# Gate and up projections of two batches in one product, attention of the last batch moved ahead, activation tables loaded at other places

## The chip, the cores and the metric

The kernel runs on one core of a Trainium2 chip. The metric is the device time of one execution in microseconds, the median of several runs. The core has a matrix engine (TensorE, "PE" in the profile, with its weight loads shown as "PEld"), a vector engine (VectorE, "DVE"), an activation engine (ScalarE, "ACT"), a general engine (GpSimd, "POOL") and a queue that issues DMAs (SyncE, "SP"). TensorE writes to eight accumulation banks (PSUM) of 128 x 512 float32; the other data is in SBUF. The engines each run their own instruction list in order and meet through semaphores.

## The reference

One decoder layer on x of 4 batches x 256 tokens x 256 channels, float32, in three parts, each behind a layer norm and added to the residual:

```
h = layernorm(x)                                  # norm 1
q, k = elu(h Wq + bq) + 1, elu(h Wk + bk) + 1     # 16 heads of 16
v = h Wv + bv
x = x + ((q (k^T v)) / (q sum(k) + eps)) Wo + bo  # linear attention, no mask
s = (ctx Wxq + bxq) (ctx Wxk + bxk)^T / 8         # 256 x 256 per batch, from the context alone
x = x + softmax(where(mask, -inf, s * layernorm(x)))          # norm 2
h = hadamard(layernorm(x) * SU_ug) / 64           # norm 3
u, g = h Wup^T * (scale * 64), h Wgate^T * (scale * 64)       # 1024 wide
x = x + (hadamard(silu(g) * u * SU_dp) / 64) Wdown^T * (scale * 64)
```

## The kernel before

Tokens are held as 8 tiles of 128 (`xs`), two per batch. Every product in float32 is made of rounded halves: an operand is split into a rounded part (`_hi`, a ScalarE copy) and what is left (`_lo`, a subtraction on VectorE or GpSimd), and three of the four combinations are added in a bank. A product with a 256-long contraction so takes 2 x 3 = 6 matmuls (`PASSES`).

TensorE's order is written out by hand. `HEAD` (line 55) lists the steps of the attention of batches 0 to 2 and what starts batch 3. Then a loop over the four batches runs eight steps `gate_up(b, j)` (GU, line 1113), each 128 of the 1024 inner columns: 6 matmuls for the gate, 6 for the up part, with a 128 x 128 weight block held in the array and the 256 tokens of one batch moving through it. The two halves fill one bank. Between these steps stand the steps that `SIDE` (line 61) names for (b, j): `ST` and `NUM` (state and numerator of the attention), `AT` (transposes), `OUT` (output projection), `T3` (transposes of the third norm), `XH` (Hadamard of the input), `WD` (Hadamard of the down weights, four matmuls of 512 columns per `pre` part, line 1095). For j = 8 and 9 they stand inside `down(b)` (line 1127), which contracts the eight inner blocks in 48 matmuls into two banks `Y`. For the last batch `down` takes its blocks in an order of its own, so that it need not wait for the last of them.

Seven banks are used in rotation in the order that `schedule()` (line 78) gives: the n-th group of results takes bank n mod 7, and TensorE waits in `take` until the group seven places before it has been read. The eighth bank holds the scores and the softmax (`probs`).

Each gate and up step is followed by a chain: ScalarE's `silu(n)` (line 511, reads the gate half into one of four buffers `sg`), VectorE's `hidden(n)` (line 820, multiplies by the up half and releases the bank), ScalarE's `h_hi(n)` (line 521), GpSimd's `h_lo(n)` (line 312), and TensorE's `down`. `silu(n)` waits for `h_lo(n-4)`, since there are four buffers.

The attention of a batch goes on with VectorE's `attend` (line 726, division), TensorE's `AT`, `at_hi` on ScalarE (line 458), `at_lo` on VectorE (line 674), `OUT`, `add_attn` (line 742), the statistics `ln_stats(2, b)` (line 637), GpSimd's `rstd_of(2, b)` (line 258), `times_score` (line 750), `logits` (line 763), ScalarE's `prob` (line 478), VectorE's `softmax` (line 774) and `ln_stats(3, b)`. Then GpSimd's `rstd_of(3, b)` and `shift_of(3, b)`, ScalarE's `normalise(3, b)` (line 421), `T3`, `x3_hi` and `x3_lo` (lines 486, 783), `XH`, `xh_hi` and `xh_lo`, and the batch is ready for its gate and up steps. `add_y(b)` (line 828) adds the down result to the residual, and SP stores it.

Where these stand among the `hidden`, `silu` and `h_lo` of the loop is written out in each engine's list. Before: `NUM(3)`, `AT(3)` and `OUT(3)` are in batch 1's steps, `XH(2)` too, `T3(3)` and `XH(3)` in batch 2's.

ScalarE holds one set of function tables at a time; exp and silu are in different sets. The loads (`ACT_TABLE_LOAD`) are placed by the compiler in front of the first instruction that needs another set, here the first exp, silu(0), prob(2), silu(8), prob(3) and silu(16).

Of the kernel before, what the change touches and what calls it, by code (L numbers as in the profile page):

```python
# [5 lines left out]
F32 = mybir.dt.float32  # L6
# [7 lines left out]
P = 128  # L14
# [45 lines left out]

SIDE = {(0, 0): (("ST", 3),), (0, 1): (("NUM", 2),), (0, 2): (("T3", 1),), (0, 3): (("WD", 0), ("WD", 1)),
# [12 lines left out]
def banks_of(group, i):  # L74
    return [(group, i, t) for t in range(2)] if group in ("NUM", "Y") else [(group, i, 0)]


def schedule():

    order = [g for name, i in HEAD for g in banks_of(name, i)]  # L80
    for b in range(BATCH):
        for j in range(JB):
            order += [("GU", JB * b + j, 0)]
            order += [g for name, i in SIDE.get((b, j), ()) for g in banks_of(name, i)]
        order += banks_of("Y", b)
        order += [g for j in (JB, JB + 1) for name, i in SIDE.get((b, j), ()) for g in banks_of(name, i)]
    return [g for g in order if g not in (("SC", 0, 0), ("SC", 1, 0))]


def decoder_kernel(nc, x, ctx_t, w_qkv, bias, w_o, w_ug, w_d, vec, row, mask_ss, mask_key, const, out):  # L90
# [8 lines left out]
    with stack:  # L99
        def sb(name, shape, dt=F32):  # L100
            return stack.enter_context(nc.sbuf_tensor(name, shape, dt))
# [9 lines left out]
        wqkv = sb("wqkv", [P, 2, 3, FB, HID], F32R)  # L111
        wo = sb("wo", [P, 2, FB, HID], F32R)
# [20 lines left out]
        exp_first = sb("exp_first", [P, TILES])  # L133
        xn = sb("xn", [P, 2, ST, HID])
# [30 lines left out]
        hs = sb("hs", [P, 2, JB, SEQ], F32R)  # L165

# [12 lines left out]
        junk = back[:, 1, 0:CHUNK // 2].bitcast(BF16)  # L179
        stage = [home[:, i, :].rearrange("p (f c) -> p f c", f=FB) for home in (front, back) for i in range(2)]  # L180
# [23 lines left out]
        def wait_read(eng, name, i, t=0):  # L204
# [12 lines left out]
                 "x3_hi xh_hi sg h_hi h_lo").split()  # L217
# [37 lines left out]
        def _(pool):  # L255
# [60 lines left out]

            g.memset(junk, 0.0).then_inc(s["junk"], 1)
# [32 lines left out]
            for n in range(JB):  # L350
                h_lo(n)
                if n == 1:
                    add_ob(2)
                if n == 4:
                    add_ob(3)
            rstd_of(2, 2)
            rstd_of(3, 2)
            shift_of(3, 2)
            for n in range(JB, 2 * JB):
                h_lo(n)  # L360
                if n == JB + 4:
                    rstd_of(2, 3)
            rstd_of(3, 3)
            shift_of(3, 3)
            for n in range(2 * JB, 4 * JB):
                h_lo(n)
# [4 lines left out]
        def _(act):  # L371
# [4 lines left out]
            a.activation(exp_first[:, :], mhalf[:, :], ACT.Exp)  # L376

# [150 lines left out]

            one_rows()
# [69 lines left out]
            for n in range(JB, 2 * JB):  # L599
                silu(n)  # L600
                if n == JB:
                    normalise(3, 2, xn3)
                else:
                    h_hi(n - 1)
                if n == JB + 2:
                    x3_hi(2)
                if n == JB + 3:
                    at_hi(3)
                if n == JB + 6:
                    xh_hi(2)  # L610
            h_hi(2 * JB - 1)
            prob(3)
            negate_mean(3, 3)
            for n in range(2 * JB, 3 * JB):
                silu(n)
                if n > 2 * JB:
                    h_hi(n - 1)
                if n == 2 * JB + 1:
                    normalise(3, 3, xn3)
                if n == 2 * JB + 3:  # L620
                    x3_hi(3)
                if n == 2 * JB + 5:
                    xh_hi(3)
            h_hi(3 * JB - 1)
            for n in range(3 * JB, 4 * JB):
                silu(n)
                if n > 3 * JB:
                    h_hi(n - 1)
            h_hi(4 * JB - 1)
# [4 lines left out]
        def _(dve):  # L634
# [274 lines left out]
            hidden(7)  # L909
            add_attn(2)  # L910
            ln_stats(2, 2)
            times_score(2)
            logits(2)
            softmax(2)
            ln_stats(3, 2)
            add_y(0)
            for n in range(JB, 2 * JB):
                hidden(n)
                if n == JB + 1:
                    attend(3)  # L920
                if n == JB + 2:
                    x3_lo(2)
                if n == JB + 3:
                    at_lo(3)
                if n == JB + 4:
                    add_attn(3)
                    ln_stats(2, 3)
                    times_score(3)
                if n == JB + 5:
                    logits(3)  # L930
                if n == JB + 6:
                    xh_lo(2)
            softmax(3)
            add_y(1)
            ln_stats(3, 3)
            for n in range(2 * JB, 3 * JB):
                hidden(n)
                if n == 2 * JB + 3:
                    x3_lo(3)
                if n == 2 * JB + 5:  # L940
                    xh_lo(3)
            add_y(2)
            for n in range(3 * JB, 4 * JB):
                hidden(n)
            add_y(3)
# [4 lines left out]
        def _(pe):  # L950
# [7 lines left out]
            def done(ins, name, i, t=0):  # L958
                ins.then_inc(full[bank_of[name, i, t]], 1)
# [166 lines left out]

            def down(b):
# [6 lines left out]
                def block_products(i, j):  # L1134
                    for n, (wa, hb) in enumerate(((1, 0), (0, 0), (0, 1))):
                        ins = mm(dst[i][:, 0:HID], hs[:, hb, j, i * P:(i + 1) * P], wdh[:, wa, j, :],  # L1136
                                 start=(j == 0 and n == 0), stop=(j == JB - 1 and n == 2))
                    return ins

                if b == BATCH - 1:  # L1140

                    for j in range(JB - 1):
                        pe.wait_ge(s["h_lo"], JB * b + j + 1)
                        block_products(0, j)
                    block_products(1, 0)
                    block_products(1, 1)
                    pe.wait_ge(s["h_lo"], JB * b + JB)
                    done(block_products(0, JB - 1), "Y", b, 0)
                    for j in range(2, JB - 1):
                        block_products(1, j)  # L1150
                    done(block_products(1, JB - 1), "Y", b, 1)
                    return
# [17 lines left out]
            for b in range(BATCH):  # L1170
# [4 lines left out]
                down(b)  # L1175

# [42 lines left out]
```

## Time and profile before

| | us |
|---|---|
| device time, median of 3 runs (132.08 to 132.5) | 132.26 |
| span of the profiled execution | 130.6 |
| TensorE busy | 123.9 (95%) |
| VectorE busy | 79.7 (61%) |
| ScalarE busy | 75.4 (58%) |
| GpSimd busy | 68.8 (53%) |

The span runs from the first to the last instruction that the profiler recorded; the device time has the launch and the end around it. Matmuls overlap, so their busy time is no measure of their pace; the pace is the distance from one to the next. "Busy" of an engine is a share of the whole span, and says nothing of a single stretch.

### The profile page before, as it was taken

What the parts mean: (1) busy time and instruction counts of PE and PEld (TensorE: products, weight loads), DVE (VectorE), ACT (ScalarE), POOL (GpSimd) and SP (SyncE); (2) the same over time, 40 slices, a digit from 0 to 9 for tenths busy, and PEclk for the clock granted to TensorE, in tenths of its full rate; (3) what the DMA queues carried; (4) which work ended last, traced back from release to release, by engine and by line L of the source; (5) the groups of instructions that cost most, each with busy time, mean ns of one, the idle gap of its engine ahead of it and who ended that gap; (6) DMA issues with size and microseconds to landing.
All of it is one profiled execution on the core that took longest, in us unless ns stands there. A gap on an engine that the chain in (4) does not pass through costs nothing.

```text
span 130.6 us, 2612 instructions
## 1 busy us (share of the span) xinstructions
PE 123.9 (95%) x974; PEld 116.0 (89%) x974; DVE 79.7 (61%) x202; ACT 75.4 (58%) x162; POOL 68.8 (53%) x89
## 2 busy tenths in 40 slices
PE   6899999996999999999999999999999999999991
PEld 2249799986999999699999999999999999999990
DVE  1279969677997794999786486662535512232211
ACT  1497639984576589668553883556496630345500
POOL 2200999889999998746270344452326350055500
PEclk9999999999999999999999999999999999999999
DMA  4999985000000000000000200000200000200011
GB/s 113 304 346 381 397 241 201 0 0 3 3 5 0 0 0 8 0 0 0 5 0 0 80 0 5 3 0 0 85 0 0 3 0 5 80 0 0 0 39 47
DMA packets 4353, 7.68 MB, mean 59 GB/s; under 512 B 560, under 2 KB 2096, under 8 KB 4212
## 3 DMA queue, kind: packets, MB, share of 16 engines
q1 hardware_dynamic: 4334, 7.50, 17.0%
q8 instruction: 8, 0.13, 0.4%
q14 instruction: 5, 0.04, 0.1%
q10 hardware_dynamic: 6, 0.01, 0.0%
HBM read 6.46 MB, written 1.05 MB: 57 GB/s over the span
## 4 chain that ended last, share of the span: by engine, by line
PE 60%; POOL 13%; DVE 11%; ACT 7%; issue 4%; DMA 3%; POOLq 0%; ACTq 0%
PE bank L1123 31%; PE bank L1136 18%; POOL wd_a L303 4%; POOL wug L309 4%; DMA x_res<-in_x 3%; PE bank L1003 3%; POOL rstd L263 2%; DVE st L644 2%; PE bank L1087 2%; PE bank L1109 2%; PE bank L1025 2%; POOL wd_b L303 2%; PE bank L1069 1%; ACT L518 1%; DVE xT L802 1%
## 5 line engine op out<-in xcount | busy, mean ns | idle before, releaser
L1123 PE MATMUL bank<-xh_home,wug 128*128 128x256 f32 x384 | 49.5, 285 | 0.3 <-DVE at L737 0.3
L1123 PEld LDWEIGHTS bank<-xh_home,wug 128*128 128x128 f32 x384 | 47.1, 191 | 0.9 <-issue 0.7
L314 POOL TENSOR_TENSOR hs<-front,hs 128x256 fp32r<-128x256 f32 x32 | 24.0, 758 | 33.1 <-ACT hs L527 33.1
L518 ACT ACTIVATE front<-bank,vecs 128x256 f32<-128x256 f32 x32 | 15.0, 472 | 20.3 <-PE bank L1123 20.1
L825 DVE SCALAR_TENSOR_TENSOR front<-bank,sc_up,front 128x256 f32<-128x256 f32 x32 | 15.2, 480 | 18.2 <-ACT front L518 18.2
L1136 PE MATMUL bank<-wdh,hs 128*128 128x256 f32 x192 | 23.7, 283 | 0.0
L1136 PEld LDWEIGHTS bank<-wdh,hs 128*128 128x128 f32 x192 | 23.3, 191 | 0.0
L527 ACT CAST hs<-front 128x256 fp32r<-128x256 f32 x32 | 12.8, 400 | 4.0 <-DVE front L825 4.0
L1025 PE MATMUL bank<-wqkv,xT 128*128 128x256 f32 x96 | 14.1, 288 | 0.1
L1025 PEld LDWEIGHTS bank<-wqkv,xT 128*128 128x128 f32 x96 | 12.2, 189 | 1.2 <-ACT xT L436 0.7
L261 POOL TENSOR_SCALAR veps<-mv 128x2 f32<-128x2 f32 x12 | 2.3, 192 | 19.8 <-DVE mv L647 19.1
L644 DVE BATCH_NORM_STATS2 st<-x_res 128x6 f32<-128x256 f32 x24 | 9.0, 416 | 3.3 <-DMA x_res<-in_x 3.1
L303 POOL TENSOR_TENSOR wd_b<-wd_a 128x1024 f32<-128x1024 f32 x4 | 9.5, 2400 | 0.1
L263 POOL TENSOR_TENSOR rstd<-veps,mhalf 128x2 f32<-128x2 f32 x12 | 8.8, 732 | 1.0
L832 DVE TENSOR_TENSOR x_res<-bank,x_res 128x256 f32<-128x256 f32 x8 | 3.1, 419 | 8.8 <-PE bank L1136 8.7
L1049 PE MATMUL bank<-xT,wqkv 128*128 128x256 f32 x48 | 7.0, 285 | 0.0
L483 ACT ACTIVATE bank<-bank,low 128x256 f32<-128x256 f32 x8 | 3.5, 443 | 5.7 <-DVE low L770 5.7
L1087 PE MATMUL bank<-wo,aT 128*128 128x256 f32 x48 | 6.4, 282 | 0.0
L1049 PEld LDWEIGHTS bank<-xT,wqkv 128*128 128x128 f32 x48 | 6.2, 189 | 0.0
L1087 PEld LDWEIGHTS bank<-wo,aT 128*128 128x128 f32 x48 | 5.9, 189 | 0.0
L770 DVE CUSTOM_DVE_ANT_0 bank<-bank,mbias,rstd 128x256 f32<-128x256 f32 x8 | 3.6, 490 | 3.2 <-POOL rstd L263 3.2
L429 ACT ACTIVATE xn<-x_res,nmr,rstd 128x256 f32<-128x256 f32 x6 | 3.3, 594 | 3.6 <-POOL nmr L270 3.6
(105 smaller groups left out, 194.1 us busy)
## 6 DMA issues: line engine op xcount, KB each, us to landing
wd_a<-in_w_d SPq DMA_DIRECT2D x1, 1024.0 KB, 8.6
front<-in_w_ug SPq DMA_DIRECT2D x2, 512.0 KB, 9.7
back<-in_w_ug SPq DMA_DIRECT2D x2, 512.0 KB, 5.0
out<-x_res SPq DMA_DIRECT2D x8, 128.0 KB, 1.9
wd_b<-in_w_qkv SPq DMA_DIRECT2D x3, 256.0 KB, 4.9
x_res<-in_x SPq DMA_DIRECT2D x1, 512.0 KB, 6.6
x_res<-in_x SPq DMA_DIRECT2D x1, 385.0 KB, 3.8
back<-in_ctx_t SPq DMA_DIRECT2D x1, 260.0 KB
```

The source lines that it names most:

```text
L263: g.tensor_tensor(rstd[:, n - 1, two], veps[:, n - 1, two], mhalf[:, 0:2], ALU.pow).then_inc(s[f"rstd{n}"], 1)
L303: g.tensor_tensor(dst[:, :, half, :], src[:, :, 0, :], src[:, :, 1, :], ALU.subtract if half else ALU.add)\
L314: g.tensor_tensor(hs[:, 1, n % JB, :], sg[:, n % RING, :], hs[:, 0, n % JB, :].bitcast(F32), ALU.subtract)\
L518: a.activation(sg[:, n % RING, :], B("GU", n)[:, 0:SEQ], ACT.Silu, scale=vecs[:, V_WSUG + JB + j:V_WSUG + JB + j + 1]).then_inc(s["sg"], 1)
L527: a.copy(hs[:, 0, n % JB, :], sg[:, n % RING, :]).then_inc(s["h_hi"], 1)
L644: v.bn_stats(st[:, n - 1, t, :], xs[:, t, :]).then_inc(s[f"stats{n}"], 1)
L825: v.scalar_tensor_tensor(sg[:, n % RING, :], B("GU", n)[:, SEQ:2 * SEQ], sc_up[:, j:j + 1], sg[:, n % RING, :], ALU.mult, ALU.mult).then_i ...
L1025: ins = mm(into, xT[:, b % 2, xb, k, i * P:(i + 1) * P], wqkv[:, wa, c, k, :], start=(n == 0), stop=(name == "V" and n == len(X_PASSES) - 1))
L1049: mm(into, wqkv[:, wa, 2, k, m * P:(m + 1) * P], xT[:, b % 2, xb, k, :], start=(n == 0), stop=False)
L1087: ins = mm(dst[:, i * HID:(i + 1) * HID], aT[:, ab, k, i * P:(i + 1) * P], wo[:, wa, k, :], start=(n == 0), stop=(n == len(X_PASSES) - 1))
L1123: ins = mm(dst[:, n * SEQ:(n + 1) * SEQ], wug[:, wa, k, at_col + j * P:at_col + (j + 1) * P], xh[b][:, xb, k, :], start=(i == 0), stop=(i ...
L1136: ins = mm(dst[i][:, 0:HID], hs[:, hb, j, i * P:(i + 1) * P], wdh[:, wa, j, :], start=(j == 0 and n == 0), stop=(j == JB - 1 and n == 2))
```

## The change

Batches 0 and 1 (`ALONE = 2`) keep their loop. Batches 2 and 3 (`PAIR`) get eight steps `gate_up_pair(j)`: 12 matmuls each, with the tokens of both batches, 512 columns, moving through one weight block. Gate and up fill a bank each (`GG`). `silu_pair`, `hidden_pair`, `h_hi_pair` and `h_lo_pair` follow; the first two work on 512 columns, the other two on each batch by itself. The two `down` of these batches stand behind all eight steps. Batch 3's inner blocks lie in the memory of the attention weights (`watt`), which are no longer needed, and the four buffers `sg2` in that of the staged gate and up weights. For the pair, batch 2 and 3 must both be through their `XH`: so `NUM(3)` and `OUT(2)` move up into batch 0's steps, `AT(3)` into `down(0)`, `OUT(3)`, `T3(2)`, `XH(2)`, `T3(3)` into batch 1's, `XH(3)` into `down(1)`. The lists of VectorE, ScalarE and GpSimd are put in a matching order: both softmaxes stand in front of the first `hidden` and `silu` of batch 1. `table(...)` is an activation of one column without any other use; it stands before `negate_mean(3, 1)` with silu and behind silu(7) with exp.

```diff
 SIDE = {(0, 0): (("ST", 3),), (0, 1): (("NUM", 2),), (0, 2): (("T3", 1),), (0, 3): (("WD", 0), ("WD", 1)),
-        (0, 4): (("AT", 2), ("WD", 2), ("WD", 3)), (0, 5): (("XH", 1),), (0, 7): (("OUT", 2),),
-        (1, 1): (("NUM", 3),), (1, 2): (("T3", 2),), (1, 3): (("AT", 3),), (1, 4): (("OUT", 3),), (1, 6): (("XH", 2),),
-        (2, 3): (("T3", 3),), (2, 5): (("XH", 3),)}
+        (0, 4): (("AT", 2), ("WD", 2), ("WD", 3)), (0, 5): (("XH", 1), ("NUM", 3)), (0, 6): (("OUT", 2),),
+        (0, JB + 1): (("AT", 3),), (1, 0): (("OUT", 3),), (1, 2): (("T3", 2),), (1, 4): (("XH", 2),),
+        (1, 7): (("T3", 3),), (1, JB): (("XH", 3),)}
@@ schedule
+    for j in range(JB):
+        order += banks_of("GG", j)
+    for b in range(ALONE, BATCH):
+        order += banks_of("Y", b)
@@ GpSimd
+            def h_lo_pair(j):
+                for i, b in enumerate(range(ALONE, BATCH)):
+                    pool.wait_ge(s["h_hi2"], 2 * j + i + 1)
+                    g.tensor_tensor(hs_of[b][:, 1, j, :], sg2[:, j % RING, i, :], hs_of[b][:, 0, j, :].bitcast(F32),
+                                    ALU.subtract).then_inc(s["h_lo2"], 1)
             for n in range(JB):
+                if n == JB - 1:
+                    rstd_of(2, 2)
                 h_lo(n)
...
-            rstd_of(2, 2)
             rstd_of(3, 2)
             shift_of(3, 2)
+            rstd_of(2, 3)
+            rstd_of(3, 3)
             for n in range(JB, 2 * JB):
                 h_lo(n)
-                if n == JB + 4:
-                    rstd_of(2, 3)
-            rstd_of(3, 3)
-            shift_of(3, 3)
-            for n in range(2 * JB, 4 * JB):
-                h_lo(n)
+                if n == JB:
+                    shift_of(3, 3)
+            for j in range(JB):
+                h_lo_pair(j)
@@ ScalarE
+            def table(function, n):
+                a.activation(table_in[:, n:n + 1], neg1[:, :], function)
+            def silu_pair(j):
+                wait_full(act, "GG", j, 0)
+                if j >= RING:
+                    act.wait_ge(s["h_lo2"], 2 * (j - RING) + 2)
+                a.activation(sg2[:, j % RING, :, :].rearrange("p b s -> p (b s)"), B("GG", j, 0)[:, :], ACT.Silu,
+                             scale=vecs[:, V_WSUG + JB + j:V_WSUG + JB + j + 1]).then_inc(read_of("GG", j, 0), 1)
+            def h_hi_pair(j):
+                wait_read(act, "GG", j, 1)
+                if j == 0:
+                    wait_full(act, "Y", ALONE - 1, 1)
+                for i, b in enumerate(range(ALONE, BATCH)):
+                    a.copy(hs_of[b][:, 0, j, :], sg2[:, j % RING, i, :]).then_inc(s["h_hi2"], 1)
...
             exp_q(3)
+            table(ACT.Silu, 0)
             negate_mean(3, 1)
...
+            table(ACT.Exp, 1)
             h_hi(JB - 1)
+            at_hi(3)
             prob(2)
             negate_mean(3, 2)
+            normalise(3, 2, xn3)
+            prob(3)
             for n in range(JB, 2 * JB):
                 silu(n)
+                if n > JB:
+                    h_hi(n - 1)
                 if n == JB:
                     x3_hi(2)
+                if n == JB + 1:
+                    negate_mean(3, 3)
                 if n == JB + 3:
                     xh_hi(2)
+                    normalise(3, 3, xn3)
             h_hi(2 * JB - 1)
+            x3_hi(3)
+            xh_hi(3)
+            for j in range(JB):
+                silu_pair(j)
+                if j:
+                    h_hi_pair(j - 1)
+            h_hi_pair(JB - 1)
@@ VectorE
+            def hidden_pair(j):
+                wait_full(dve, "GG", j, 1)
+                wait_read(dve, "GG", j, 0)
+                both = sg2[:, j % RING, :, :].rearrange("p b s -> p (b s)")
+                v.scalar_tensor_tensor(both, B("GG", j, 1)[:, :], sc_up[:, j:j + 1], both, ALU.mult, ALU.mult)\
+                    .then_inc(read_of("GG", j, 1), 1)
...
             hidden(6)
-            hidden(7)
             add_attn(2)
             ln_stats(2, 2)
             times_score(2)
+            attend(3)
+            hidden(7)
             logits(2)
+            at_lo(3)
             softmax(2)
             ln_stats(3, 2)
+            add_attn(3)
+            ln_stats(2, 3)
+            times_score(3)
             add_y(0)
+            logits(3)
+            softmax(3)
+            ln_stats(3, 3)
             for n in range(JB, 2 * JB):
                 hidden(n)
+                if n == JB:
                     x3_lo(2)
                 if n == JB + 3:
                     xh_lo(2)
+            x3_lo(3)
+            xh_lo(3)
             add_y(1)
+            for j in range(JB):
+                hidden_pair(j)
+            for b in range(ALONE, BATCH):
+                add_y(b)
@@ TensorE
+            def gate_up_pair(j):
+                if j == 0:
+                    for b in range(ALONE, BATCH):
+                        wait_read(pe, "XH", b)
+                for n, at_col in enumerate((INTER, 0)):
+                    dst = take("GG", j, n)
+                    for i, (k, wa, xb) in enumerate(PASSES):
+                        cols = slice(xb * FB * SEQ + k * SEQ, xb * FB * SEQ + (k + 1) * SEQ)
+                        ins = mm(dst[:, :].rearrange("p (b s) -> p b s", s=SEQ), wug[:, wa, k, at_col + j * P:at_col + (j + 1) * P],
+                                 xh_home[:, PAIR, cols], start=(i == 0), stop=(i == len(PASSES) - 1))
+                    done(ins, "GG", j, n)
+            def down_pair():
+                for b in range(ALONE, BATCH):
+                    for i in range(ST):
+                        dst = take("Y", b, i)
+                        for j in range(JB):
+                            if b == ALONE and i == 0:
+                                pe.wait_ge(s["h_lo2"], 2 * j + 1)
+                            if b == ALONE + 1 and i == 0:
+                                pe.wait_ge(s["h_lo2"], 2 * j + 2)
+                            ins = block_products(dst, b, i, j)
+                        done(ins, "Y", b, i)
```

## Rows read from the trace of the kernel before

**Rows 1.** The page: TensorE's busy time; the granted clock in 40 slices, tenths.

```profile
PE 123.9 (95%) x974; PEld 116.0 (89%) x974; DVE 79.7 (61%) x202; ACT 75.4 (58%) x162; POOL 68.8 (53%) x89
...
PEclk9999999999999999999999999999999999999999
```

**Rows 2.** Windows: busy us and count per engine, granted clock, DMA share, GB/s.

```profile
45.00:92.00 47.00, 46.56 (x383) 45.36 (x382) 34.41 (x88) 30.53 (x65) 24.01 (x31) 1.00 0.02 7
```

**Rows 3.** Chain that ended last: start us, us, engine, line, count; pieces from 54 us.

```profile
54.60 0.14 issue
...
56.85 0.92 PE bank L1095 x4
...
63.04 1.41 PE bank L1087 x12
...
73.08 0.93 PE bank L1069 x8
...
75.44 0.44 PE bank L1003 x4
...
110.53 11.52 PE bank L1123 x96
```

**Rows 4.** Timeline of TensorE: start us, us, line, operands, count, idle before and releaser.

```profile
32.43 0.63 PE L1003 MATMUL bank<-x_res,at 128*128 128x128 f32 x4 [1.09 <-DVE at L737]
...
54.74 1.68 PE L1123 MATMUL bank<-xh_home,wug 128*128 128x256 f32 x12 [0.30 <-DVE at L737]
...
60.00 3.04 PE L1123 MATMUL bank<-xh_home,wug 128*128 128x256 f32 x24
...
64.28 5.92 PE L1136 MATMUL bank<-wdh,hs 128*128 128x256 f32 x48
...
77.44 0.63 PE L1003 MATMUL bank<-x_res,at 128*128 128x128 f32 x4
```

**Rows 5.** Groups of instructions by line and shape: busy, mean ns, idle before.

```profile
L314 POOL TENSOR_TENSOR hs<-front,hs 128x256 fp32r<-128x256 f32 x32 | 24.0, 758 | 33.1 <-ACT hs L527 33.1
...
L825 DVE SCALAR_TENSOR_TENSOR front<-bank,sc_up,front 128x256 f32<-128x256 f32 x32 | 15.2, 480 | 18.2 <-ACT front L518 18.2
...
L527 ACT CAST hs<-front 128x256 fp32r<-128x256 f32 x32 | 12.8, 400 | 4.0 <-DVE front L825 4.0
...
L456 ACT ACTIVATE eq<-bank,neg 128x512 f32<-128x512 f32 x4 | 2.7, 686 | 0.3 <-PE bank L1050 0.3
```

**Rows 6.** Timeline of ScalarE at 46 us, and VectorE's `at_lo(2)`.

```profile
45.90 0.70 ACT L456 ACTIVATE eq<-bank,neg 128x512 f32<-128x512 f32 x1
47.08 0.20 ACT L384 ACTIVATE nmean<-mv 128x2 f32<-128x2 f32 x1 [0.49 <-DVE mv L647]
...
48.25 1.28 ACT L518 ACT_TABLE_LOAD   x1
...
60.58 0.69 DVE L676 TENSOR_TENSOR aT<-bank,aT 128x512 fp32r<-128x512 f32 x1 [0.25 <-ACT aT L462]
```

**Rows 7.** Timeline of VectorE and ScalarE: the steps from residual to statistics, and `at_hi(3)`.

```profile
65.22 0.68 DVE L746 TENSOR_TENSOR x_res<-bank,x_res 128x512 f32<-128x512 f32 x1
...
67.04 0.89 DVE L759 SCALAR_TENSOR_TENSOR bank<-x_res,mv,score 128x256 f32<-128x256 f32 x2
...
68.12 0.49 DVE L770 CUSTOM_DVE_ANT_0 bank<-bank,mbias,rstd 128x256 f32<-128x256 f32 x1 [0.19 <-POOL rstd L263]
...
69.11 0.45 ACT L483 ACTIVATE bank<-bank,low 128x256 f32<-128x256 f32 x1 [2.06 <-DVE low L770]
...
71.82 0.30 DVE L647 BATCH_NORM_AGGREGATE mv<-st 128x2 f32<-128x6 f32 x2
72.04 0.72 DVE L832 TENSOR_TENSOR x_res<-bank,x_res 128x256 f32<-128x256 f32 x2
...
78.11 0.59 ACT L462 CAST aT<-bank 128x512 fp32r<-128x512 f32 x1
```

**Rows 8.** Timeline of VectorE: one `x3_lo`.

```profile
99.07 0.69 DVE L785 TENSOR_TENSOR x3T<-bank,x3T 128x512 fp32r<-128x512 f32 x1 [0.29 <-ACT x3T L490]
```

More of the change, by code:

```diff
@@ L58 @@
         ("XH", 0), ("V", 3), ("Q", 3), ("ST", 2))
+ALONE = 2
+PAIR = slice(ALONE, BATCH)
 SIDE = {(0, 0): (("ST", 3),), (0, 1): (("NUM", 2),), (0, 2): (("T3", 1),), (0, 3): (("WD", 0), ("WD", 1)),
[3 rows of a table removed]
+        (0, 4): (("AT", 2), ("WD", 2), ("WD", 3)), (0, 5): (("XH", 1), ("NUM", 3)), (0, 6): (("OUT", 2),),
+        (0, JB + 1): (("AT", 3),), (1, 0): (("OUT", 3),), (1, 2): (("T3", 2),), (1, 4): (("XH", 2),),
+        (1, 7): (("T3", 3),), (1, JB): (("XH", 3),)}
 def hadamard(n):
@@ L74, in banks_of @@
 def banks_of(group, i):
-    return [(group, i, t) for t in range(2)] if group in ("NUM", "Y") else [(group, i, 0)]
+    return [(group, i, t) for t in range(2)] if group in ("NUM", "Y", "GG") else [(group, i, 0)]
 def schedule():
     order = [g for name, i in HEAD for g in banks_of(name, i)]
-    for b in range(BATCH):
+    for b in range(ALONE):
         for j in range(JB):
@@ L110, in decoder_kernel @@
         xs = first[:, X_AT:].rearrange("p (t d) -> p t d", d=HID)
-        wqkv = sb("wqkv", [P, 2, 3, FB, HID], F32R)
-        wo = sb("wo", [P, 2, FB, HID], F32R)
+        watt = sb("watt", [P, 2 * JB * SEQ], F32R)
+        wqkv = watt[:, 0:6 * FB * HID].rearrange("p (l c f o) -> p l c f o", l=2, c=3, f=FB)
+        wo = watt[:, 6 * FB * HID:].rearrange("p (l f o) -> p l f o", l=2, f=FB)
         mx = sb("mx", [CTX1, CTX1])
@@ L133, in decoder_kernel @@
         exp_first = sb("exp_first", [P, TILES])
+        table_in = sb("table_in", [P, 2])
         xn = sb("xn", [P, 2, ST, HID])
@@ L165, in decoder_kernel @@
         hs = sb("hs", [P, 2, JB, SEQ], F32R)
+        hs_of = [hs[:, :, :, :]] * (ALONE + 1) + [watt[:, :].rearrange("p (l j s) -> p l j s", l=2, j=JB)]
         early = hs[0:CTX1, :, :, :].rearrange("p l j s -> p (l j s)").rearrange("p (w l t) -> p w l t", w=2, l=2)
@@ L179, in decoder_kernel @@
         junk = back[:, 1, 0:CHUNK // 2].bitcast(BF16)
+        sg2 = back[:, :, :].rearrange("p l s -> p (l s)").rearrange("p (r b s) -> p r b s", r=RING, b=BATCH - ALONE)
         stage = [home[:, i, :].rearrange("p (f c) -> p f c", f=FB) for home in (front, back) for i in range(2)]
@@ L216, in decoder_kernel @@
                  "sx logit prob rsum x2 "
-                 "x3_hi xh_hi sg h_hi h_lo").split()
+                 "x3_hi xh_hi sg h_hi h_lo h_hi2 h_lo2").split()
         s = {n: sem("s_" + n) for n in names}
@@ L595, in _ @@
                     xh_hi(1)
+            table(ACT.Exp, 1)
             h_hi(JB - 1)
+            at_hi(3)
             prob(2)
             negate_mean(3, 2)
+            normalise(3, 2, xn3)
+            prob(3)
             for n in range(JB, 2 * JB):
                 silu(n)
+                if n > JB:
+                    h_hi(n - 1)
                 if n == JB:
[L602 to L605, printed above, removed]
                     x3_hi(2)
+                if n == JB + 1:
+                    negate_mean(3, 3)
                 if n == JB + 3:
-                    at_hi(3)
-                if n == JB + 6:
                     xh_hi(2)
+                    normalise(3, 3, xn3)
             h_hi(2 * JB - 1)
[L612 to L629, printed above, removed]
+            x3_hi(3)
[5 more added lines that the diff above has]
+            h_hi_pair(JB - 1)
         @block.vector
@@ L912, in _ @@
             times_score(2)
+            attend(3)
+            hidden(7)
             logits(2)
+            at_lo(3)
             softmax(2)
             ln_stats(3, 2)
+            add_attn(3)
+            ln_stats(2, 3)
+            times_score(3)
             add_y(0)
+            logits(3)
+            softmax(3)
+            ln_stats(3, 3)
             for n in range(JB, 2 * JB):
                 hidden(n)
-                if n == JB + 1:
-                    attend(3)
-                if n == JB + 2:
+                if n == JB:
                     x3_lo(2)
                 if n == JB + 3:
[L924 to L931, printed above, removed]
                     xh_lo(2)
-            softmax(3)
+            x3_lo(3)
+            xh_lo(3)
             add_y(1)
[L935 to L945, printed above, removed]
+            for j in range(JB):
+                hidden_pair(j)
+            for b in range(ALONE, BATCH):
+                add_y(b)
         @block.tensor
@@ L1125, in gate_up, with block_products @@
                 done(ins, "GU", JB * b + j)
+            def gate_up_pair(j):
[9 more added lines that the diff above has]
+                    done(ins, "GG", j, n)
+            def block_products(dst, b, i, j):
+                for n, (wa, hb) in enumerate(((1, 0), (0, 0), (0, 1))):
+                    ins = mm(dst[:, 0:HID], hs_of[b][:, hb, j, i * P:(i + 1) * P], wdh[:, wa, j, :],
+                             start=(j == 0 and n == 0), stop=(j == JB - 1 and n == 2))
+                return ins
             def down(b):
@@ L1132, in down @@
                         wait_read(pe, "WD", n)
[L1134 to L1152, printed above, removed]
                 for i in range(ST):
@@ L1156, in down @@
                             pe.wait_ge(s["h_lo"], JB * b + j + 1)
-                        block_products(i, j)
+                        block_products(dst[i], b, i, j)
                     for name, n in SIDE.get((b, JB + i), ()):
@@ L1161, in down @@
                 for i in range(ST):
-                    done(block_products(i, JB - 1), "Y", b, i)
+                    done(block_products(dst[i], b, i, JB - 1), "Y", b, i)
+            def down_pair():
[9 more added lines that the diff above has]
+                        done(ins, "Y", b, i)
             steps = {"mx": weights_product, "u": project, "T1": turn1, "SC": scores, "K": k_proj, "V": v_proj, "Q": q_proj,
@@ L1169, in _ @@
                 steps[name](i)
-            for b in range(BATCH):
+            for b in range(ALONE):
                 for j in range(JB):
@@ L1175, in _ @@
                 down(b)
+            for j in range(JB):
+                gate_up_pair(j)
+            down_pair()
 def kernel(**inputs):
```

## The prediction

> **What bounds the kernel now.** I read the page first. TensorE is busy 95% of the span at the full granted clock, VectorE 61%, ScalarE 58%, GpSimd 53% [rows 1]. Then the stages: from 45 to 92 us TensorE is busy 46.56 of 47.00 us [rows 2]. Then the chain of waits: from 54.74 us to the end it is one run of TensorE pieces, closed by one VectorE add [rows 3]. So a matmul taken away after 45 us is time won, and a microsecond in which TensorE waits is lost whole. The timeline shows few waits there: 0.30 us at 54.74 and a late start at 77.44, both behind the division in `attend` (L737); a longer one, 1.09 us, stands earlier at 32.43 [rows 4]. The chain also gives the pace of products, a piece over its count: 128 columns 0.44/4 = 110 ns, 136 columns 0.93/8 = 116 ns, 256 columns 11.52/96 = 120 ns, 512 columns 0.92/4 = 230 ns [rows 3].
>
> **Part 1, the paired gate and up products.** Batches 2 and 3 issue 16 blocks of 12 products with 256 columns: 192 x 0.120 = 23.04 us. They become 96 products of 512 columns. The one row of that width is the four products of L1095, 230 ns each: 96 x 0.230 = 22.08, which saves 0.96 us. The reason is in the same rows: from 128 to 256 columns the pace rises by 10 ns only, so up to there something paid once per product (its weight load) sets it; from 256 to 512 it rises by 110 ns, near the 107 ns of 256 more columns at 2.4 GHz. At 256 columns the weight load is already almost hidden, and halving the number of loads buys little. Bounds: below, 512 columns at 2.4 GHz, 213 ns, saves 2.56 us; above, twice the 256-column pace, saves nothing. I take 0.96, a measured row of this width and type, though of four products only. The Trainium skill, "TensorE: Matmul & The Clock Gate", section "Back-to-back issue gap", gives a sustained 131 ns per 512-column product in a stream of weight loads and products; by it the phase would take 96 x 0.131 = 12.6 us and save 10.4. The trace's 230 ns speaks against it, so it stays a rival with a small chance.
>
> Do the other engines keep up? A pair takes TensorE 24 half-width products' worth, 2.76 us. ScalarE: one 512-wide activation from a bank (0.69, as L456) and two rounding copies at 0.40, 1.49 us. GpSimd: 2 x 0.758 = 1.52. VectorE under 0.7 [rows 5]. All hidden. The old down product of batch 3 reordered its blocks for the last residual; the new one begins with 21 products, 2.52 us. From the last product's end: 0.2 until it is seen, multiply 0.69, copy 0.40, subtraction 0.76, but GpSimd still works on block 6 until about 1.4, so it ends near 2.2. That is 0.3 inside the 2.52, so no stall. The last group of products, add and store are the same. I cost the tail at nothing.
>
> **Part 2, table loads.** Before, ScalarE ends `exp_q(3)` at 46.60, negates a mean at 47.08, copies, and loads the silu table at 48.25 for 1.28 us; the rest (`normalise`, `pre_hi(1)`, VectorE's `pre_lo(1)`, `hidden(1)`, `attend(2)`) leads straight to TensorE's wait at 54.74 [rows 4, 6]. Moved, the load starts at 46.60, followed by a one-column activation of about 0.2; the mean then comes at about 48.1, 1.0 late, and what followed the load is only 1.28 - 1.0 = 0.3 earlier. It removes the 0.30 wait: -0.3. The exp load is put behind silu(7), where ScalarE waits for `hidden(7)` and `at_hi(3)` anyway: nothing. The silu load before silu(8) stays, now behind the softmax of batch 3, where it runs beside VectorE's statistics.
>
> **Part 3, attention of batch 3 early.** The tensor work is moved, not changed. What changes is what it waits for.
>
> (a) `NUM(3)` takes two banks, so GU(6) now takes the bank of AT(2), freed by `at_lo(2)`. Before, that ended at 60.58 + 0.69 = 61.27 [rows 6], now 60.97, and with 0.14 from release to product, as at 54.60 [rows 3], it is 61.1. TensorE arrives at 60.00 - 0.3 + 0.93 = 60.63 [rows 3, 4]: a wait of 0.47 us. `down(0)` starts at 64.28 - 0.3 + 0.93 + 0.47 = 65.4.
>
> (b) `AT(3)` sits inside `down(0)` behind 42 products, 5.04 us: 70.4. VectorE's program has `at_lo(3)` in front of `softmax(2)`, ScalarE's has `at_hi(3)` in front of `prob(2)`. So the softmax of batch 2, which began at 69.11 before, now waits for AT(3); behind it, one after the other, stand the statistics of 2, the residual, statistics and scores of 3, the add of Y(0), logits, softmax and statistics of 3, and only then `hidden(8)`. On ScalarE silu(8) waits behind `prob(3)`. The spacings are those of batch 2 before. Transposes to `at_hi`: 78.11 - 77.44 = 0.67, so 71.05 (at_hi); `prob(2)` 0.57 later, 71.6. From prob to the end of the statistics 72.12 - 69.11 = 3.01: 74.6. OUT(3), 1.41 behind GU(8), is done by then. From `add_attn` to the end of `times_score` 67.93 - 65.22 = 2.71: 77.3. `add_y(0)` 0.72 with small overlaps: first half 77.7, both 77.95. Logits to prob 69.11 - 68.12 = 0.99: 78.94. Prob to statistics 3.01: 81.95. `hidden(8)` 0.48: 82.4 [rows 4, 5, 7]. The table load runs from 80.0 to 81.3 and is not last.
>
> TensorE meanwhile ends `down(0)` at 70.4 + 0.44 + 0.72 = 71.56. XH(2) takes the bank of GU(8), which `hidden(8)` frees: 82.5. Before XH(2) TensorE has five blocks (7.20), OUT(3) 1.41 and T3(2) 0.44, 9.05 us in all [rows 3]: it would be there at 80.6. So it loses **1.9 us**, some 0.5 of it already at T3(2), whose bank is that of Y(0,0), freed by `add_y(0)`. Then XH(2)'s third product needs `x3_lo(2)`, 0.68 long and behind `hidden(8)` [rows 8], two products less: 0.36 more. Of XH(3) in `down(1)`: `x3_hi(3)` stands behind ScalarE's backlog (two instructions per block, about 0.85 us, against 1.44 on TensorE, so caught up by 90.6), `x3_lo(3)` ends at 91.3 against 91.1: 0.1. GpSimd's `rstd_of(3,3)`, now in front of `h_lo(8)`, waits until 82; silu(12), first to need that buffer, is later than this on ScalarE. What goes: the late start of AT(3) at 77.44, 0.3, since `attend(3)` now ends at 69. XH(3) is ready before the pair phase.
>
> **Sum.** -0.96 - 0.3 + 0.47 + 1.9 + 0.36 + 0.1 - 0.3 = +1.27 us. The profiled span is 130.6; with 1.27 it is 131.8. The runs' median, 132.26, lies 1.7 above the span, launch and end included, and I keep that: 133.5 us. The bounds of the unknown costs: the pair phase -2.56 to 0, the chain of (b) +-0.6 (some twenty hand-offs taken from one batch), the two small stalls 0 to 0.6.
>
> **Rivals.** A: the 512-column product runs at 213 ns. For it: the first of only four intervals may be disturbed, and no long stream stands in the trace. Against: 256 columns also stay 13 ns above their 107. It gives 132.26 + 1.27 - 1.60 = 131.9. By the Trainium skill's 131 ns of that section, 96 x 0.099 less than forecast, it would be near 124.
>
> B, other side: VectorE and ScalarE clear the chain before TensorE needs bank 2; for it, TensorE has 9 us of other work between `down(0)` and XH(2), and these engines are only some 60% busy; against, the 12 us from AT(3) to `hidden(8)` are a chain of dependent steps. It decides where the chain is under 10.2 us; then 1.9 and 0.36 go, 131.2 us, faster. C: the chain is longer, because GpSimd (its pow for two rstd's) or buses add 1 us: 134.5. D: TensorE's clock falls to 1.2 GHz behind the wait. After the 1.09 us wait at 32.43 it was still granted in full [rows 1, 4]; mine is up to 1.4 us in a piece. The 48 products from XH(2) to T3(3) at 213 instead of 120 ns would be 4.5 us: 138.
>
> **How the numbers follow.** Forecast, slower by some 0.2 to 2.2 us: 0.62. A 0.12, a pace of 131 ns 0.01, B 0.12, C 0.11, D 0.02. What a measurement can tell from no change is 0.3%, 0.4 us, so 131.86 to 132.66. Faster than that: the 131 ns case 0.01, A's lower part 0.05, most of B 0.08, together 0.14. Same: the rest of A 0.07, a B that clears only part of the wait 0.04, the low edge of the forecast 0.05, together 0.16. Slower: the rest of the forecast 0.57, C 0.11, D 0.02, 0.70. The range reaches down to A and up past C and leaves out most of B and D: 131.9 to 134.7.
>
> **What would show it.** In the trace after: products of the pair phase 230 ns apart; TensorE waiting about 0.5 us at GU(6), 0.5 at T3(2), over 1 us at XH(2), with VectorE's multiply (`hidden`) as the releaser; no wait at GU(4); VectorE's first `hidden` of batch 1 near 82 us; no wait in the last 30 us. If the pair phase takes 20.5 us or XH(2) starts without a wait, the forecast is wrong.

## The result, and the profile after

The changed kernel takes 134.76 us in the median against 132.20 of the kernel before; the ratio of the two is 1.0181 (95% interval 1.0145 to 1.0217), or 2.4 us slower. The span of its profiled execution is 133.0 us, against 130.6. The forecast was 133.5 us, slower, in a range to 134.7: the sign came out, and the time lies at the upper end of the range (134.76 as measured, 134.6 by the ratio), with a loss nearly twice the 1.27 us of the forecast. (Single executions of several kernels were about 2% longer than the rest, and one of e8 took 674 us; these are left out of all ratios.)

TensorE's pieces in the chain that ended last (start us, us, engine, line, count) answer to [rows 3]; L1166 is `gate_up_pair`, L1172 `down`, L1126 `WD`:

```profile
57.88 0.92 PE bank L1126 x4
...
96.91 21.79 PE bank L1166 x96
118.69 11.51 PE bank L1172 x96
```

The wide products stand 21.79/96 = 227 ns apart, where the four of the kernel before gave 230. The pair phase lasts 21.79 us in place of 192 x 0.120 = 23.04. The last 33 us before the final add hold no wait. So the pairing gave 1.25 us, and what was lost lies before 96.7 us. The timeline of TensorE there (start us, us, line, operands, count, idle before and who ended it), the waits that answer to [rows 4]:

```profile
52.81 1.70 PE L1154 MATMUL bank<-xh_home,wug 128*128 128x256 f32 x12 [0.90 <-DVE front L857]
...
55.78 1.66 PE L1154 MATMUL bank<-xh_home,wug 128*128 128x256 f32 x12 [0.30 <-DVE at L769]
...
62.36 1.69 PE L1154 MATMUL bank<-xh_home,wug 128*128 128x256 f32 x12 [0.19 <-DVE aT L708]
...
66.76 5.20 PE L1172 MATMUL bank<-wdh,hs 128*128 128x256 f32 x42
...
79.24 0.66 PE L1034 MATMUL bank<-x_res,front 128*128 128x128 f32 x4 [0.27 <-DVE x_res L871]
79.65 3.11 PE L1154 MATMUL bank<-xh_home,wug 128*128 128x256 f32 x24
83.83 1.61 PE L1140 MATMUL bank<-x3T,had_x 128*128 128x256 f32 x8 [1.08 <-DVE front L857]
85.28 4.48 PE L1154 MATMUL bank<-xh_home,wug 128*128 128x256 f32 x36
...
92.55 1.12 PE L1140 MATMUL bank<-x3T,had_x 128*128 128x256 f32 x8
93.50 3.40 PE L1172 MATMUL bank<-wdh,hs 128*128 128x256 f32 x27
```

The reader sees three forecast waits: GU(6) behind `at_lo(2)` at 62.36, T3(2) behind `add_y(0)` at 79.24, XH(2) behind `hidden(8)` at 83.83. The bracket counts idle time of a pipelined engine and is shorter than what is lost; from start to start, 79.65 + 24 x 0.120 = 82.53 is where XH(2) would have begun, so 1.30 us are lost, and its eight products take 1.45 us (to 85.28), where those of XH(3) take 0.95 (92.55 to 93.50). The fourth wait, 0.90 us at GU(3), was not forecast, and the one at GU(4), which the forecast had gone, is still there, at 55.78 in place of 54.74.

Its cause is on VectorE. First the kernel before, then the changed one, VectorE and GpSimd from 48 to 50 us; L802 and L834 are `pre_lo(0)`, L309 and L322 `ug_lo(3)`, L270 and L283 `shift_of(3, 1)`:

```profile
48.26 1.22 DVE L802 TENSOR_TENSOR xh_home<-wd_b,xh_home 128x1024 fp32r<-128x1024 f32 x1 [0.27 <-ACT xh_home L504]
48.84 0.70 POOL L270 TENSOR_TENSOR nmr<-nmean,rstd 128x2 f32<-128x2 f32 x1
49.50 2.40 POOL L309 TENSOR_TENSOR wug<-back,wug 128x1024 fp32r<-128x1024 f32 x1
```

```profile
48.73 0.19 POOL L283 TENSOR_TENSOR nmr<-nmean,rstd 128x2 f32<-128x2 f32 x1
48.88 2.40 POOL L322 TENSOR_TENSOR wug<-back,wug 128x1024 fp32r<-128x1024 f32 x1
49.06 3.30 DVE L834 TENSOR_TENSOR xh_home<-wd_b,xh_home 128x1024 fp32r<-128x1024 f32 x1 [1.18 <-ACT xh_home L528]
```

The same subtraction takes 1.22 us in one and 3.30 in the other. Before, VectorE started first, GpSimd's tiny multiply of 0.19 took 0.70 and ended 0.06 us behind VectorE's, and `ug_lo(3)` ran after it. After, VectorE's input is ready 0.18 us behind the start of `ug_lo(3)`, and VectorE's 3.30 are what is left of GpSimd's instruction, 51.28 - 49.06 = 2.22, and its own 1.1. Both read two operands from SBUF. So whichever of the two engines started second was held until the other's instruction had ended. The Trainium skill, "SBUF — State Buffer", section "Who interferes with whom", says that a VectorE instruction with two SBUF inputs contends with a GpSimd instruction that reads SBUF, that the port pair which they share is an exclusive lock, and that the order of issue decides who is blocked. By that rule the trace agrees, both ways round.

### The profile page after: what moved, and what is told of

Its sections match the earlier page's. It is cut to its first block, busy times and chain, and to the rows that moved or that the text cites. A ratio compares the mean times of both kernels' runs of the same rounds, so it can differ in the third digit from the quotient of the medians.

```text
span 133.0 us, 2398 instructions
## 1 busy us (share of the span) xinstructions
PE 124.1 (93%) x878; PEld 111.6 (84%) x878; DVE 80.4 (60%) x194; ACT 70.6 (53%) x154; POOL 68.3 (51%) x89
## 4 chain that ended last, share of the span: by engine, by line
PE 53%; DVE 15%; POOL 12%; ACT 7%; issue 7%; DMA 3%; SPq 0%; ACTq 0%; DVEq 0%; POOLq 0%
PE bank L1172 17%; PE bank L1166 16%; PE bank L1154 9%; POOL wd_a L316 4%; POOL wug L322 4%; DMA back<-in_ctx_t 3%; PE bank L1118 2%; DVE st L676 2%; PE bank L1034 2%; PE bank L1056 2%; POOL wd_b L316 2%; POOL rstd L276 2%; PE bank L1140 1%; ACT wug L500 1%; ACT bank L507 1%
## 5 line engine op out<-in xcount | busy, mean ns | idle before, releaser
L1154 PE MATMUL bank<-xh_home,wug 128*128 128x256 f32 x192 | 25.6, 286 | 1.4 <-DVE front L857 0.9
L1166 PE MATMUL bank<-xh_home,wug 128*128 128x512 f32 x96 | 22.0, 389 | 0.0
L1166 PEld LDWEIGHTS bank<-xh_home,wug 128*128 128x128 f32 x96 | 18.0, 188 | 3.7
L327 POOL TENSOR_TENSOR hs<-front,hs 128x256 fp32r<-128x256 f32 x16 | 12.4, 788 | 12.7 <-ACT hs L551 12.7
L1172 PE MATMUL bank<-wdh,hs 128*128 128x256 f32 x144 | 18.3, 284 | 0.0
L1172 PEld LDWEIGHTS bank<-wdh,hs 128*128 128x128 f32 x144 | 17.7, 190 | 0.2
L864 DVE SCALAR_TENSOR_TENSOR back<-bank,sc_up,back 128x512 f32<-128x512 f32 x8 | 6.0, 751 | 16.1 <-PE bank L1166 16.1
L1056 PE MATMUL bank<-watt,xT 128*128 128x256 f32 x96 | 14.2, 289 | 0.1
L1056 PEld LDWEIGHTS bank<-watt,xT 128*128 128x128 f32 x96 | 12.4, 190 | 1.2 <-ACT xT L460 0.7
L542 ACT ACTIVATE front<-bank,vecs 128x256 f32<-128x256 f32 x16 | 7.6, 474 | 5.3 <-PE bank L1154 5.3
L551 ACT CAST hs<-front 128x256 fp32r<-128x256 f32 x16 | 6.5, 404 | 4.7 <-DVE front L857 4.7
L857 DVE SCALAR_TENSOR_TENSOR front<-bank,sc_up,front 128x256 f32<-128x256 f32 x16 | 7.6, 476 | 2.1 <-ACT front L542 2.0
L1080 PE MATMUL bank<-xT,watt 128*128 128x256 f32 x48 | 7.0, 285 | 0.0
```

Of the source, the lines that this page charges most:

```text
L327: g.tensor_tensor(hs[:, 1, n % JB, :], sg[:, n % RING, :], hs[:, 0, n % JB, :].bitcast(F32), ALU.subtract)\
L542: a.activation(sg[:, n % RING, :], B("GU", n)[:, 0:SEQ], ACT.Silu, scale=vecs[:, V_WSUG + JB + j:V_WSUG + JB + j + 1]).then_inc(s["sg"], 1)
L551: a.copy(hs[:, 0, n % JB, :], sg[:, n % RING, :]).then_inc(s["h_hi"], 1)
L857: v.scalar_tensor_tensor(sg[:, n % RING, :], B("GU", n)[:, SEQ:2 * SEQ], sc_up[:, j:j + 1], sg[:, n % RING, :], ALU.mult, ALU.mult).then_i ...
L1056: ins = mm(into, xT[:, b % 2, xb, k, i * P:(i + 1) * P], wqkv[:, wa, c, k, :], start=(n == 0), stop=(name == "V" and n == len(X_PASSES) - 1))
L1080: mm(into, wqkv[:, wa, 2, k, m * P:(m + 1) * P], xT[:, b % 2, xb, k, :], start=(n == 0), stop=False)
```

## The experiments

**One term at a time: the early silu load.** e1 is the changed kernel without it, e2 the kernel before with it alone.

```diff
 # e1, on the changed kernel        # e2, on the kernel before
             exp_q(3)
-            table(ACT.Silu, 0)      (e1)
+            a.activation(table_in[:, 0:1], neg1[:, :], ACT.Silu)      (e2)
             negate_mean(3, 1)
```

> The changed kernel without its early activation with silu, so that the silu table is loaded in front of silu(0) as before. Theory (port): the early load made pre_hi(0) late, VectorE's pre_lo(0) then met GpSimd's ug_lo(3) and took 3.30 us in place of 1.22; without it pre_lo(0) takes about 1.2 us, the product waits at 52.8 us goes, GU(4) starts near 54.8 in place of 55.8, and the time falls by about 1.0 us, to 133.7. Rival (my forecast's working): the early load saved 0.3 us, so without it the time rises by 0.3 us.

> The kernel before with one edit, the one-column silu activation in front of negate_mean(3, 1). Theory (port): pre_lo(0) starts 0.1 to 0.2 us behind ug_lo(3) and takes 3.3 us; GU(4) starts 1.0 us later; time 132.2 + 1.0 = 133.2. Rival (forecast): 0.3 us faster than before, 131.9.

e1: 133.76 us, ratio to before 1.0078 (1.0046 to 1.0109), so 1.4 us below the changed kernel by the ratios. e2: 133.65 us, ratio 1.0081 (1.0038 to 1.0125), 1.1 us slower than before by one instruction. In e2's timeline GpSimd again starts first, and GU(4), last row, is late:

```profile
48.70 2.39 POOL L310 TENSOR_TENSOR wug<-back,wug 128x1024 fp32r<-128x1024 f32 x1
...
48.87 3.30 DVE L804 TENSOR_TENSOR xh_home<-wd_b,xh_home 128x1024 fp32r<-128x1024 f32 x1 [1.18 <-ACT xh_home L505]
...
55.59 1.19 PE L1125 MATMUL bank<-xh_home,wug 128*128 128x256 f32 x8 [0.31 <-DVE at L739]
```

In e1 the row is the old one, the subtraction 1.22 us and GU(4) at 54.40:

```profile
47.92 1.22 DVE L833 TENSOR_TENSOR xh_home<-wd_b,xh_home 128x1024 fp32r<-128x1024 f32 x1 [0.27 <-ACT xh_home L528]
...
54.40 1.67 PE L1153 MATMUL bank<-xh_home,wug 128*128 128x256 f32 x12 [0.31 <-DVE at L768]
```

The traces do not all start alike: in those used here the first transposes of TensorE begin between 6.82 and 7.44 us, long before any edit acts. So positions are best compared as distances from a common row. From GU(0) (45.08 us in the changed kernel) to GU(4) it is 10.70 us in the changed kernel and 10.68 in e2, both with the early load, and 9.63 in the kernel before and 9.55 in e1, both without it: 1.0 to 1.15 us. Both exclude my working, by which the load saved 0.3 us.

**Is it the exclusion?** e3 leaves VectorE's and ScalarE's lists as they are and makes GpSimd start later.

```diff
             shift_of(3, 1)
+            pool.wait_ge(s["pre_lo"], 1)
             ug_lo(3)
```

> The changed kernel, with GpSimd made to wait for VectorE's pre_lo(0) before ug_lo(3). Theory (port, held for a whole instruction by whoever starts first): pre_lo(0) falls from 3.30 to 1.22 us although VectorE's own program is untouched; ug_lo(3) starts near 50.3 and ends near 52.7, so that pre_lo(1), ready at 51.4, is now the one that is long (about 2.5 us). TensorE's wait at 52.8 goes, GU(4) starts near 55.5; time about 0.3 us below the changed kernel. Rival (the operand of pre_lo(0) or something else in VectorE is slow): pre_lo(0) stays at 3.3 us.

134.36 us, ratio 1.0129 (1.0066 to 1.0193), 0.7 us below the changed kernel by the ratios, with intervals that overlap, so the times do not show a gain; the trace decides:

```profile
49.02 1.23 DVE L835 TENSOR_TENSOR xh_home<-wd_b,xh_home 128x1024 fp32r<-128x1024 f32 x1 [1.18 <-ACT xh_home L529]
...
50.33 2.40 POOL L322 TENSOR_TENSOR wug<-back,wug 128x1024 fp32r<-128x1024 f32 x1 [1.42 <-DVE xh_home L835]
...
51.32 2.50 DVE L835 TENSOR_TENSOR xT<-wd_b,xT 128x1024 fp32r<-128x1024 f32 x1 [0.33 <-ACT xT L529]
...
55.37 1.30 PE L1155 MATMUL bank<-xh_home,wug 128*128 128x256 f32 x9 [0.31 <-DVE at L770]
```

The first subtraction is at 1.23 again, with nothing changed on VectorE, and the second, which had taken 1.21, is now the long one: it waits out `ug_lo(3)` in its turn and ends at 53.82, 1.09 us behind it (1.08 in the changed kernel and in e2). GU(4) is 10.32 us from GU(0), 0.38 less than in the changed kernel. That is the exclusion, and the rival (an operand or an instruction that is slow by itself) is out.

**The wide products alone.** e4 keeps the schedule and issues each 512-column product as two.

```diff
-                        ins = mm(dst[:, :].rearrange("p (b s) -> p b s", s=SEQ), wug[...], xh_home[:, PAIR, cols], ...)
+                    for h, b in enumerate(range(ALONE, BATCH)):
+                        for i, (k, wa, xb) in enumerate(PASSES):
+                            ins = mm(dst[:, h * SEQ:(h + 1) * SEQ], wug[...], xh[b][:, xb, k, :], ...)
```

> The changed kernel with each 512-column product of the pair phase issued as two of 256 columns, 192 in place of 96, all else the same. Theory: the pair phase takes 192 x 0.120 = 23.0 in place of 21.8 us, time 1.25 us above the changed kernel, 135.9. Rival: the pace was not what the pairing gained (waits in the phase), difference under 0.5 us.

136.33 us, ratio 1.0275 (1.0211 to 1.0339), so 1.2 us above the changed kernel. The chain has one piece for it:

```profile
97.18 23.04 PE bank L1166 x192
```

23.04 less 21.79 is 1.25: the pairing is worth this, and nothing else of the change is in it.

**The wait at XH(2).** e5 and e6 let ScalarE and VectorE serve GU(8) before the softmax of batch 3 is done; e5 on the changed kernel, e6 on e1.

```diff
 # ScalarE
             prob(2)
+            silu(JB)
             negate_mean(3, 2)
             normalise(3, 2, xn3)
+            silu(JB + 1)
+            table(ACT.Exp, 1)
+            x3_hi(2)
             prob(3)
...
 # VectorE
             logits(3)
+            x3_lo(2)
+            hidden(JB)
             softmax(3)
 (the moved steps leave their old places, in the loops behind)
```

> The changed kernel with the softmax region reordered: ScalarE runs silu(8) and silu(9) between prob(2) and prob(3) (one more table load each way) and x3_hi(2) in front of prob(3); VectorE runs x3_lo(2) and hidden(8) while ScalarE does prob(3). Theory (TensorE's wait at XH(2) is for GU(8)'s bank, kept by hidden(8) behind the whole softmax chain): the wait of 1.3 us at 83.8 and the 0.5 us inside XH(2) go; ScalarE's later list gives back some of it; time 0.8 to 1.8 us below the changed kernel, 133.3. Rival (the chain itself, not the place of hidden(8), is the bound, and the wait only moves to the next bank): under 0.4 us gained.

> Both: without the early silu activation, and with the reordering of e5. If the two losses are independent terms of one sum, the gains add: 134.6 - 1.0 - 1.3 = 132.3, level with the kernel before. Rival: they overlap, and it stays near 133.3.

Both missed their expectations. e5: 135.00 us, ratio 1.0207 (1.0178 to 1.0236), no faster than the changed kernel's 1.0181. e6: 133.85 us, ratio 1.0124 (1.0097 to 1.0152), no faster than e1's 1.0078. That the early load costs the same on top of the reordering (1.0207 against 1.0124, 1.1 us) does hold. e6's trace shows where the gain went, TensorE and ScalarE:

```profile
81.89 1.12 PE L1141 MATMUL bank<-x3T,had_x 128*128 128x256 f32 x8
...
83.02 0.20 ACT L408 ACTIVATE nmean<-mv 128x2 f32<-128x2 f32 x1 [1.45 <-DVE mv L680]
...
83.24 1.28 ACT L542 ACT_TABLE_LOAD   x1
...
88.43 3.25 PE L1173 MATMUL bank<-wdh,hs 128*128 128x256 f32 x21 [0.49 <-issue]
91.52 1.50 PE L1141 MATMUL bank<-x3T,had_x 128*128 128x256 f32 x8
...
96.09 21.95 PE L1167 MATMUL bank<-xh_home,wug 128*128 128x512 f32 x96
```

The wait at XH(2) is gone: it follows GU(12) at once. But my order put `negate_mean(3, 3)` in front of silu(10): ScalarE stands 1.45 us for the statistics, and the silu load, which needs nothing, comes only then. Its list is late from there on, and TensorE pays at T3(3), `down(1)` and XH(3): from XH(2) to the first pair product 14.20 us, where the work alone is about 12.4.

e8 was e6 with NUM(3) behind GU(6) and OUT(3) in front of GU(8), to take away the waits at GU(6) and T3(2) as well. It was expected at 131.6 us and missed too: 133.56 us, ratio 1.0100 (1.0063 to 1.0137). Both waits are gone from its trace, but from XH(2) to the first pair product it takes 14.49 us (80.94 to 95.43), no less than in e6.

**That list mended.** e9 is e6 with silu(10) right behind `prob(3)`, so that silu(10) and `h_hi(8)` both stand in front of `negate_mean(3, 3)` (`h_hi(8)` already did in e6), and with NUM(3) behind GU(6), which e7 tries by itself on e1. e10 also puts OUT(3) in front of GU(8), and so is e8 with silu(10) moved and nothing else.

```diff
 # e7, e9, e10: SIDE
-        ... (0, 5): (("XH", 1), ("NUM", 3)), (0, 6): (("OUT", 2),),
+        ... (0, 5): (("XH", 1),), (0, 6): (("NUM", 3), ("OUT", 2)),
 # e9 against e6, e10 against e8: ScalarE, the loop written out
             prob(3)
+            silu(JB + 2)
             h_hi(JB)
             negate_mean(3, 3)
-            silu(JB + 2)
             h_hi(JB + 1)
 # e10: SIDE, with the steps of (0, JB + 2) run behind down(0)
-        (1, 0): (("OUT", 3),),
+        (0, JB + 2): (("OUT", 3),),
```

> Without the early silu activation, and with NUM(3) behind GU(6) in place of in front of it, so that GU(6) takes another bank than AT(2)'s. Theory: the wait behind at_lo(2), 0.3 to 0.4 us, goes; time 0.35 us below e1, 133.3. Rival: at_lo(2) delays OUT(2) or the chain behind it all the same, no gain.

> e6 with NUM(3) behind GU(6), and on ScalarE silu(10) and h_hi(8) in front of negate_mean(3, 3), so that the silu table is loaded right behind prob(3) and not behind a wait of 1.45 us for the statistics. Theory (in e6 TensorE's wait at XH(2) was gone, and the 1.3 us were lost again to ScalarE's late list: T3(3), down(1), XH(3)): the stretch from XH(2) to the first pair product falls from 14.2 to about 12.4 us; time 1.8 us below e6 for this and 0.35 for GU(6), 131.8. Rival (ScalarE's list is too full with two more table loads, whatever the order): above 133.

> e9 with OUT(3) in front of GU(8), which takes away TensorE's wait at T3(2) (0.4 us) and costs up to 0.3 us inside OUT(3): 0.1 us below e9, not to be told from it.

e7: 133.11 us, ratio 1.0070 (1.0043 to 1.0097). Against e1's 1.0078 (1.0046 to 1.0109) the expected 0.35 us, 0.3% of the time, can be neither shown nor excluded. The trace shows it: the wait at GU(6) is gone. XH(2) starts at 82.46, and in e1 at 82.43, which looks like no gain; but e7's profiled execution was late from its first transposes on, at 7.40 us against 6.90. Counted from there, AT(3) comes after 63.03 us against 63.51, and XH(2) after 75.06 against 75.53. So the trace has 0.47 us for this step, and the runs leave it open.

e9: 131.67 us, ratio 0.9943 (0.9915 to 0.9971), by the ratios 0.7 us faster than the kernel before and 3.1 faster than the changed one. e10: 131.96, ratio 0.9967 (0.9942 to 0.9992), not to be told from e9, as expected. Against e8's 1.0100 it is 1.8 us faster by the ratios, for the place of silu(10) alone. e9's rows:

```profile
78.27 3.12 PE L1156 MATMUL bank<-xh_home,wug 128*128 128x256 f32 x24
81.22 1.12 PE L1142 MATMUL bank<-x3T,had_x 128*128 128x256 f32 x8
82.18 4.48 PE L1156 MATMUL bank<-xh_home,wug 128*128 128x256 f32 x36
...
89.47 1.49 PE L1142 MATMUL bank<-x3T,had_x 128*128 128x256 f32 x8
...
94.02 21.95 PE L1168 MATMUL bank<-xh_home,wug 128*128 128x512 f32 x96
```

```profile
80.30 1.28 ACT L542 ACT_TABLE_LOAD   x1
81.60 0.48 ACT L542 ACTIVATE front<-bank,vecs 128x256 f32<-128x256 f32 x1
81.97 0.40 ACT L551 CAST hs<-front 128x256 fp32r<-128x256 f32 x1
82.37 0.20 ACT L408 ACTIVATE nmean<-mv 128x2 f32<-128x2 f32 x1
```

The load now stands right behind `prob(3)`, and the mean needs no wait. From XH(2) to the first pair product it is 12.80 us, and that product starts at 94.02, against 95.33 in e1; counted from the first transposes (7.33 and 6.90 us) it comes 1.74 us sooner. What is left is the wait at T3(2) and 0.4 us in XH(3).

## Why the prediction was right in sign, and what it missed

The terms from start to start in the trace, forecast and measured:

| step | forecast us | measured us | how |
|---|---|---|---|
| pair phase | -0.96 | -1.25 | 21.79 against 23.04; e4 |
| table load in front of `negate_mean(3, 1)` | -0.3 | +1.0 | GU(4) 55.78 against 54.74; e1, e2 |
| GU(6) behind `at_lo(2)` | +0.47 | +0.5 | `down(0)` 66.76 - 64.28 - 1.04 - 0.93 (NUM(3)); e7 |
| T3(2) and XH(2) behind the softmax chain | +1.9 | +1.7 | 0.42 + 1.30 |
| inside XH(2), `x3_lo(2)` | +0.36 | +0.5 | 85.28 - 83.83 - 0.95 |
| XH(3) | +0.1 | 0 | 92.55 to 93.50 |
| late start of AT(3) gone | -0.3 | -0.3 | no wait in front of it |
| sum | +1.27 | +2.2 | span +2.4; some 0.2 us is not assigned |

**The mechanism of part 3 (b) was right, and so was its size.** `hidden(8)` was to end at 82.4 us, 12.0 after the start of AT(3) at 70.4. It ends at 83.33 + 0.45 = 83.78, 11.99 after AT(3):

```profile
71.79 0.60 PE L1034 MATMUL bank<-x_res,at 128*128 128x128 f32 x4
...
83.33 0.45 DVE L857 SCALAR_TENSOR_TENSOR front<-bank,sc_up,front 128x256 f32<-128x256 f32 x1
```

One link was another than forecast: in the chain `add_attn(3)`, at 76.13, stands behind OUT(3), which ended at 76.11, and not behind the softmax of batch 2, since OUT(3) was not done before it as I had it. The spacings of batch 2 in [rows 7] carried over to batch 3, and so did the nine microseconds of other work of TensorE. Rival B, which held that this work would cover the chain, fell here. e6 and e9 show that the place of `hidden(8)` in VectorE's list, and not the chain, kept XH(2) waiting: there it starts at once.

**The step that failed is part 2.** I counted the 1.28 us that left ScalarE's list and the 1.0 by which what came before the old place was later, and followed the path through `pre_hi(1)`. On that path the gain came: ScalarE's `normalise(3, 1)` starts at 49.30 in place of 49.91. The path through `pre_hi(0)` and `pre_lo(0)`, 0.8 us later, the prediction does not mention; by itself it would have cost next to nothing, since in e3, where `pre_lo(0)` is short, `hidden(0)` starts at 50.17 against 50.05 before. But `pre_lo(0)` now starts behind `ug_lo(3)` and not in front of it, and became 2.1 us longer. e1 and e2 measure this term at 1.1 to 1.4 us lost in device time, against 0.3 saved in the forecast. Together that is 1.4 to 1.7 us, more than the 1.1 between 133.5 and the 134.6 that the ratio gives; the pair phase and the smaller wait at XH(2) gave part of it back. That the time came out at the end of the range and not beyond it is in part luck: these errors have opposite signs (+1.3 against -0.3 and -0.2 in the table).

The rows that would have told me were in the trace of before: a GpSimd multiply of 128 x 2 took 0.70 us where its kind takes 0.19, and ended 0.06 us behind VectorE's subtraction.

**The pair phase** was taken 0.3 us too dear, from a row of four products. At 256 columns the pace is 120 ns, 13 above the 107 of the columns alone; at 512 it is 227, 14 above 213. The excess is paid per product, so half the products save half of it: 96 x 13 ns = 1.25 us, which e4 gives back. Rival A (213 ns) and the figure of 131 ns both fall: the latter would have made this phase 12.6 us, and it is 21.79. TensorE's clock was granted in full throughout (mean 1.000), with a wait of 1.30 us in it, so rival D fell; rival C came near the time with its 134.5, but not for its own reason, since the chain took its forecast 12.0 us.

## What to carry to other kernels

When a step is moved by less than a microsecond, list not only who waits for it but who runs beside it at its new time: here an order of two instructions on engines that share no data turned over, and cost four times what the move was to gain. Merging two products of 256 columns into one of 512 saved here the fixed 13 ns of one of the two, and no more; that is to be weighed against every wait that the merged schedule needs. An instruction that waits for nothing, such as a table load, can be put in front of the next one that does wait (e9 against e6, e10 against e8), if what it makes later meets nothing new (e2). And a trace is compared with another by distances from a common row: a start that was 0.5 us later hid all of e7's gain.

## What the runs showed of the hardware that I had not expected

A VectorE subtraction of 128 x 1024 with both operands in SBUF took 1.22 us alone and 3.30 us (2.50 in e3) when a GpSimd subtraction of that kind had started before it, and ended 1.08 to 1.09 us behind GpSimd's; the other way round a GpSimd multiply of two columns took 0.70 in place of 0.19 us, and `h_lo(0)`, started 0.25 us behind VectorE's `pre_lo(1)`, 1.57 in place of 0.74. VectorE's instructions with one operand in a bank were not lengthened: beside the same `ug_lo` the kernel before ran `hidden(0)` at 50.05 and a multiply with a bank as one input at 50.45 at the usual 0.48 and 0.43 us. An exp or silu load took 1.28 us each time, and the next ScalarE instruction, where it had nothing to wait for, began 10 to 20 ns after it (load from 80.30, silu at 81.60 in e9).
